# Reusing the first pair's stored weight operands in the second, and seven block products for the last down projection

## The chip, the cores and the metric

One core of one Trainium2 chip. The time is device microseconds of one execution of the whole program, from launch to the end. The four sequences of the problem are all computed on this core.

## The reference, cut to what matters

For each of 4 sequences x (512 rows by 512 features): attention with Wq, Wk, Wv, Wp gives `attn_out`; then a first two-layer block `cms = gelu(attn_out @ cW1 + cb1) @ cW2 + cb2 + onehot(code)`, a second one `modifier = gelu([attn_out, cms] @ mW1 + mb1) @ mW2 + mb2`, and `y0 = clip(x + cms + modifier, 0, 1)`. Both have 2048 hidden features; cW1 has 512 input rows, mW1 has 1024. After them come three small expert layers (512 to 256 to 512 with gelu, residual and layer norm), chosen for each sequence by an index. All is float32. The change touches the two blocks in the middle, called layer one (cW) and layer two (mW) here.

## The kernel before, in words

**Split arithmetic.** A float32 operand is held as a high part (a cast to the fast fp32r type, on ScalarE) and a low part (operand less high part, on VectorE), each of its own. Every product is three matmuls (`mm3`, L554 to L559): high times high, high times low, low times high. Data lie transposed, features on partitions.

**Pairs and chunks.** Sequences go in two pairs. For each pair the 2048 hidden features of a layer are done in four chunks, so a pair has eight chunks (`NCHUNK`): four of layer one, four of layer two; the two pairs have chunks 0 to 7 and 8 to 15 (`NCH` is 16). A chunk first does two quads of the up projection, then the down projection of what they gave (L702 to L705, with `up_quad` and `down_chunk`).

**Up projection by seven products.** A quad is a block matrix product of 2 by 2 blocks: two tiles of hidden features, two halves of the input features, two sequences. It is done with seven block products (P1 to P7, Strassen's way in Winograd's form) instead of eight; each is two steps of k, so 6 matmuls of 128 by 512. For this the weights are summed and split into seven operands of 128 partitions by 256 in high and low part (2 KB a partition). Layer two has twice the input features, so its quad has 14 operands. A chunk thus has 14 operand steps in layer one and 28 in layer two, 84 and 168 matmuls.

**How a weight operand is made.** SyncE loads a raw piece (`raw_piece`, L426, 512 KB), VectorE makes the sums (`weight_sums`, L1226), ScalarE the high part (`weight_hi`, L897), VectorE the low part (`weight_lo`, L1222), into a ring of six (`ring`, 192 KB to 204 KB of the partition). TensorE waits for `aop_lo` at each step and counts `aop_used` after it. The making runs five steps ahead (`AHEAD`). Both pairs use the same weights, and the whole of it is done again for the second pair.

**Down projection.** `down_chunk` (L690) takes eight steps d of 12 matmuls: four tiles of hidden features, two sequences, four output tiles, no sums, 96 matmuls in all. The weights of a tile are loaded raw (`down_weights`, L432, 256 KB), split by `down_weight_hi` and `down_weight_lo`; gelu's output is split by `g_hi` (L939) and `g_lo` (L1287) into three buffers. Down step d = 7 needs `g_lo(ci, 7)`, and ScalarE does `g_hi(ci, 7)` in its own d = 5, behind `weight_hi` of the next chunk's fifth operand in d = 4 (L1023 to L1031). Results are added into `res` by VectorE (`down_add`).

**SyncE's order.** All DMAs of the kernel are issued by SyncE, from one written-out order (L384 to L548): it waits for a semaphore, issues, and goes on to the next; what stands behind a wait waits too. At the change of pairs (chunk 7) it loads the second pair's seven row operands (`next_a_operand`, 1 MB each) and x of the first pair (`xs[0]`, 2 MB, L474). In chunk 9 it stores y0 of the first pair (2 MB, L477), and in chunk 11 that in split form (4 MB, L480). Near the end of chunk 15 it loads y0_split (2 x 2 MB), x of the second pair, y0 and the weights of the first expert units (L461 to L530), with twelve `unit_columns` of 5 KB each. At the start, behind the load of the expert indices, it begins a chain for the expert weights: load a piece (`prep`, L419), high part on ScalarE (`piece_hi`, L813), low part on GpSimd, store (L415); ScalarE does its parts between those of the attention (L847 to L851).

## Time and profile before

| | |
|---|---|
| median of 3 runs | 1193.47 us (1193.29 to 1194.72) |
| the profiled execution's own time | 1194.04 us |
| its span, first to last instruction | 1192.2 us |
| TensorE matmul busy | 1178.7 us, 99% |
| VectorE, ScalarE busy | 790.8 us (66%), 569.3 us (48%) |
| DMA, mean over the span | 122 GB/s, 145.82 MB |
| granted clock, mean | 0.999 of full |

The profiled execution's time is 0.57 us over the median; its span leaves 1.8 us of it outside the first and last instruction. Busy time of TensorE is modelled at its ends, so 99% says that it hardly ever stood idle.

### The profile page before, as it was taken

To read this page: it belongs to the slowest core of one execution; us is meant where nothing else is said; L and a number is where in the kernel's file an instruction comes from. 1 tells how busy PE (TensorE), PEld (TensorE's weight loads), DVE (VectorE), ACT (ScalarE), POOL (GpSimd) and SP (SyncE) were. 2 spreads that over 40 slices of the span, in tenths; PEclk is the share of its full clock that TensorE was granted. 3 is DMA by queue.
4 is the path that set the end of the run, shared out by engine and by line. 5 is a ranking of instruction groups with operands and counts; after the bars stand their busy time and mean duration, and the time that the engine had idled before them with its cause. 6 is when DMAs were issued, how large, how long until landed. Compare 5 with 4: busy or idle time off the path is not lost.

```text
span 1192.2 us, 15272 instructions
## 1 busy us (share of the span) xinstructions
PE 1178.7 (99%) x5328; PEld 973.9 (82%) x5328; DVE 790.8 (66%) x1460; ACT 569.3 (48%) x1068; POOL 162.5 (14%) x145
## 2 busy tenths in 40 slices
PE   9999999999999999999999999999999999999997
PEld 7888878888888788888888888878888888788886
DVE  6344486776678756565667686696656565877885
ACT  5434353563544534342435643554343434357886
POOL 1332230000000000000000000000000000349981
PEclk9999999999999999999999999999999999999999
DMA  6764452124320302020561321411111118746644
GB/s 226 273 216 161 164 175 94 54 60 153 124 96 28 107 13 95 10 98 8 194 258 53 124 62 45 178 53 53 54 53 54 54 36 326 223 142 224 218 167 169
DMA packets 50610, 145.82 MB, mean 122 GB/s; under 512 B 6356, under 2 KB 6356, under 8 KB 46310
## 3 DMA queue, kind: packets, MB, share of 16 engines
q1 hardware_dynamic: 50534, 144.84, 34.7%
q8 instruction: 43, 0.70, 0.2%
q14 instruction: 33, 0.27, 0.1%
HBM read 108.11 MB, written 36.71 MB: 121 GB/s over the span
## 4 chain that ended last, share of the span: by engine, by line
PE 92%; DVE 5%; issue 1%; DMA 1%; ACT 1%; POOL 0%; POOLq 0%; DVEq 0%; SPq 0%; ACTq 0%
PE psum L557 89%; PE psum L777 2%; DVE c_op L1334 1%; DVE res L1362 1%; DVE ring L1224 1%; DVE res L1307 1%; PE psum L608 0%; PE psum L591 0%; PE psum L721 0%; PE psum L604 0%; DMA wqk_raw<-wqk_dram 0%; DVE sm L1477 0%; DMA prep<-wdu_dram 0%; DVE z L1471 0%; DVE c_t L1319 0%
## 5 line engine op out<-in xcount | busy, mean ns | idle before, releaser
L557 PE MATMUL psum<-g_hl,w_hl 128*128 128x512 f32 x1536 | 351.3, 389 | 0.4 <-DVE w_hl L1285 0.4
L557 PEld LDWEIGHTS psum<-g_hl,w_hl 128*128 128x128 f32 x1536 | 288.1, 188 | 61.0 <-DVE w_hl L1285 0.8
L557 PE MATMUL psum<-a_op,ring 128*128 128x512 f32 x1344 | 316.7, 389 | 0.7 <-DVE w_t L1266 0.7
L557 PEld LDWEIGHTS psum<-a_op,ring 128*128 128x128 f32 x1344 | 252.1, 188 | 54.0 <-DVE w_t L1266 1.5
L906 ACT CAST ring<-asum 128x256 fp32r<-128x256 f32 x192 | 77.2, 404 | 210.5 <-PE psum L557 160.0
L557 PE MATMUL psum<-c_op,ring 128*128 128x512 f32 x672 | 163.9, 391 | 0.8 <-DVE c_op L1334 0.6
L557 PEld LDWEIGHTS psum<-c_op,ring 128*128 128x128 f32 x672 | 125.5, 188 | 29.4 <-DVE c_op L1334 3.6
L1292 DVE TENSOR_TENSOR g_hl<-g,g_hl 128x512 fp32r<-128x512 f32 x128 | 88.2, 689 | 67.9 <-ACT g_hl L946 66.5
L1553 POOL TENSOR_TENSOR yT<-res,yT 128x512 fp32r<-128x512 f32 x8 | 11.7, 1488 | 846.3 <-ACT yT L1044 846.3
L1224 DVE TENSOR_TENSOR ring<-asum,ring 128x256 fp32r<-128x256 f32 x192 | 80.5, 421 | 56.1 <-ACT ring L906 54.9
L946 ACT CAST g_hl<-g 128x512 fp32r<-128x512 f32 x128 | 78.3, 618 | 77.5 <-PE psum L557 77.5
L923 ACT ACTIVATE g<-g,sm 128x512 f32<-128x512 f32 x96 | 69.5, 724 | 78.8 <-DVE g L1272 31.5
L1224 DVE TENSOR_TENSOR ring<-rawp,ring 128x256 fp32r<-128x256 f32 x144 | 60.7, 423 | 62.8 <-ACT ring L906 61.6
L906 ACT CAST ring<-rawp 128x256 fp32r<-128x256 f32 x144 | 57.6, 404 | 55.3 <-PE psum L557 55.3
L1307 DVE TENSOR_TENSOR res<-psum,res 128x512 f32<-128x512 f32 x96 | 64.8, 691 | 20.2 <-PE psum L557 18.6
L557 PE MATMUL psum<-wu,h_hl 128*128 128x512 f32 x288 | 68.4, 393 | 0.0
L557 PE MATMUL psum<-yT,wd 128*128 128x512 f32 x288 | 67.8, 391 | 0.0
L1545 POOL TENSOR_TENSOR prep<-prep 128x512 f32<-128x512 f32 x36 | 50.2, 1401 | 126.4 <-ACT prep L817 126.4
L557 PEld LDWEIGHTS psum<-yT,wd 128*128 128x128 f32 x288 | 53.8, 188 | 11.1
L557 PEld LDWEIGHTS psum<-wu,h_hl 128*128 128x128 f32 x288 | 53.3, 188 | 10.7
L1285 DVE TENSOR_TENSOR w_hl<-wraw,w_hl 128x512 fp32r<-128x512 f32 x64 | 44.1, 689 | 20.3 <-ACT w_hl L937 19.3
L557 PE MATMUL psum<-vp_w,xT 128*128 128x512 f32 x192 | 45.3, 391 | 0.0
(128 smaller groups left out, 1352.7 us busy)
## 6 DMA issues: line engine op xcount, KB each, us to landing
rawp<-up_w_dram SPq DMA_DIRECT2D x48, 512.0 KB, 3.6
wdu_split<-prep SPq DMA_DIRECT2D x36, 512.0 KB, 2.9
wraw<-dn_w_dram SPq DMA_DIRECT2D x64, 256.0 KB, 3.3
wd<-wdu_split SPq DMA_DIRECT2D x12, 1024.0 KB, 9.1
wu<-wdu_split SPq DMA_DIRECT2D x12, 1024.0 KB, 5.4
prep<-wdu_dram SPq DMA_DIRECT2D x36, 256.0 KB, 3.3
second_pair_operands<-c_op SPq DMA_DIRECT2D x7, 1024.0 KB, 6.3
a_op<-second_pair_operands SPq DMA_DIRECT2D x7, 1024.0 KB, 11.7
```

What stands on the lines that cost most here:

```text
L557: ins = nc.tensor.matmul(ps, lw(el), rw(er), start=first and i == 0, stop=last and i == 2, skip_group_check=skip)
L777: ins = nc.tensor.transpose(tr_bank(u, d)[:, i * P:(i + 1) * P], z[u % 3][:, i, d * P:(d + 1) * P], ident[:, :])
L906: nc.scalar.copy(ring[n % RING][:, 0, :], aop_src(n)).then_inc(aop_hi, 1)
L923: nc.scalar.activation(dst, src, ACT.Gelu, bias=(cb1, mb1)[l][:, t:t + 1]).then_inc(gelu_done, 1)
L946: nc.scalar.copy(g_hl[t % GHL][:, 0, :], g[:, q, 2 * row + seq, :]).then_inc(g_hi_done, 1)
L1224: nc.vector.tensor_tensor(ring[n % RING][:, 1, :], aop_src(n), f(ring[n % RING][:, 0, :]), ALU.subtract).then_inc(aop_lo, 1)
L1285: nc.vector.tensor_tensor(w_hl[t % 2][:, 1, :], wraw[t % 2][:, :], f(w_hl[t % 2][:, 0, :]), ALU.subtract).then_inc(w_lo_done, 1)
L1292: nc.vector.tensor_tensor(g_hl[t % GHL][:, 1, :], g[:, q, 2 * row + seq, :], f(g_hl[t % GHL][:, 0, :]), ALU.subtract).then_inc(g_lo_done, 1)
L1307: nc.vector.tensor_tensor(dst, bank[4 * seq + m], dst, ALU.add).then_inc(d_evac, 1)
L1334: nc.vector.tensor_tensor(c_ops[i][:, 1, :, :], src, f(c_ops[i][:, 0, :, :]), ALU.subtract).then_inc(op_lo[2 + p], 1)
L1362: nc.vector.tensor_scalar(res[:, 2 + seq, m, :], res[:, 2 + seq, m, :], 0.0, 1.0, ALU.max, ALU.min).then_inc(y0_done, 1)
L1545: nc.gpsimd.tensor_tensor(prep[i][:, 1, :], prep[i][:, 1, :], prep[i][:, 0, :], ALU.subtract).then_inc(p_lo, 1)
```

## The change: what it does

1. In the first pair every weight operand of the up projection, once split, is also stored to DRAM (`store_operand`, 168 stores of 256 KB, 2 KB rows). Its slot in the ring may be filled again only when the store has landed.
2. In the second pair (chunks 8 to 15) these operands are not made again: `load_operands` brings two at a time into the ring (512 KB, 4 KB rows), when the two that were in their place have been used. TensorE waits for the landing.
3. In chunks 8 to 11 ScalarE and VectorE make instead the operands of mW2 for the block products of the down projection (56 of them) in four staging buffers, which are stored as well.
4. In chunks 12 to 15 the down projection is done by seven block products over 2 by 2 blocks: 14 steps of 6 matmuls (84) instead of 96; the row operands are sums of gelu's output (`g_sum`), split into eight buffers (`dg`); VectorE adds the products to `acc_u` and `res`. VectorE adds `acc_u` in at the end.
5. SyncE's order follows from this: stores in all chunks of the first pair and chunks 8 to 11, loads between them. x of the first pair is loaded in four parts in chunk 8 (steps k = 4 to 7), y0 stored in four in chunk 9 (k = 0 to 3), y0_split stored in eight of 512 KB in chunk 10 (k = 1 to 8); y0_split's second half comes after chunk 15's seventh down step. The twelve `unit_columns` are issued at the start, behind the expert indices. `x_add` and the clip of the second pair's y0 come after the first rows of y0.

The diff, cut to its core:

```diff
+CS = NCHUNK + NCHUNK // 2
+LOADED = AOP
+PREPARED = AOP + PROD * QL
+UP_OPS = QC * 2 * PROD
+DOWN_STEPS = (tuple((i, 0) for i in (P1, P6, P7, P5)) + tuple((i, 1) for i in (P1, P6, P7, P5))
+              + tuple((i, q) for i in (P2, P4, P3) for q in range(QC)))
+CSTEP = len(DOWN_STEPS)
+COPS = UP_OPS + CSTEP
+TOTAL = PREPARED + (NCH - CS) * COPS
+STG = 4
+DG = 8
+ADDS = (P1, P6, P7, P5, P2, P4, P3)
+ADD_BANK = (0, 2, 4, 6, 0, 4, 6)
...
+        ring_all = at("ring", 192, [P, RING, 2, 2 * P], F32R)
+        ring = [ring_all[:, i, :, :] for i in range(RING)]
+        stage = [at(f"stage{i}", 104 + 2 * i, [P, 2, 2 * P], F32R) for i in range(STG)]
+        t_x, t_y = (at(f"t_{n}", 120 + 4 * i, [P, QC, S]) for i, n in enumerate("xy"))
+        acc_u = at("acc_u", 172, [P, 2, S])
+        dg = [at(f"dg{i}", k, [P, 2, S], F32R) for i, k in enumerate((160, 164, 168, 144, 148, 152, 112, 116))]
+        xs = [at(f"xs{i}", k, [P, 2, DT, S]) for i, k in enumerate((56, 48))]
...
+        up_ops = nc.dram_tensor("up_operands", (AOP // 2, P, 2, 4 * P), F32).ap()
+        down_ops = nc.dram_tensor("down_operands", (PROD * QL // 2, P, 2, 4 * P), F32).ap()
...
+        G_SUM_UP = {2: ((0, 0),), 3: ((0, 1),), 4: ((0, 2),), 10: ((0, 3),)}
+        G_SUM_DOWN = {1: ((1, 0), (1, 1), (1, 2)), 5: ((1, 3),)}
+        G_OP_UP = {4: 0, 6: 1, 7: 2, 8: 3, 13: 4}
+        G_OP_DOWN = {1: (5,), 2: (6,), 3: (7,), 4: (8,), 5: (9,), 6: (10,), 7: (11,), 8: (12,), 9: (13,)}
+        ADD_AT = {5: 0, 6: 1, 7: 2, 8: 3, 10: 4, 12: 5}
...
+            for u in range(LAYERS * B):
+                unit_columns(u)
...
+            def store_operand(n):
+                sp.wait_ge(aop_lo, n + 1)
+                src = f(aop_dst(n)[:, :, :].rearrange("p e n -> p (e n)"))
+                if n < LOADED:
+                    sp.dma_start(up_ops[n // 2, :, n % 2, :], src).then_inc(s_wst[n % RING], 16)
+                else:
+                    i = down_place(n)
+                    sp.dma_start(down_ops[i // 2, :, i % 2, :], src).then_inc(s_dst[n % STG], 16)
+            def load_operands(r):
+                sp.wait_ge(aop_used, r - RING + 2)
+                down, i = loaded_from(r)
+                for k in range(2):
+                    if r < LOADED + RING:
+                        sp.wait_ge(s_wst[(r + k) % RING], 16 * (LOADED // RING))
+                    if down:
+                        n = made_as(i + k) - LOADED
+                        sp.wait_ge(s_dst[n % STG], 16 * (n // STG + 1))
+                    else:
+                        sp.wait_ge(s_wst[(i + k) % RING], 16 * ((i + k) // RING + 1))
+                sp.dma_start(f(ring_all[:, r % RING:r % RING + 2, :, :].rearrange("p a e n -> p a (e n)")), (up_ops, down_ops)[down][i // 2]).then_inc(s_ring[r % RING // 2], 16)
...
+                for n in range(first, first + ops):
+                    store_operand(n)
+                    pieces_after(n)
+                    if n == first + ops - 3:
+                        down_weights(4 * ci + 2)
...
+            for r in range(LOADED, LOADED + RING, 2):
+                load_operands(r)
+            for i in (P2, P4, P3):
+                next_a_operand(NCHUNK - 1, i)
+            def x_piece(k):
+                if k == 0:
+                    sp.wait_ge(aop_used, used_after(NCHUNK - 1, 1, P6))
+                sp.dma_start(xs[0][:, k // 2, k % 2 * 2:k % 2 * 2 + 2, :], xin[k // 2, :, k % 2 * 2:k % 2 * 2 + 2, :]).then_inc(s_xs[0], 16)
+            def y0_piece(k):
+                sp.wait_ge(y0_done, k + 1)
+                sp.dma_start(y0_dram[:, k // 2, k % 2 * 2:k % 2 * 2 + 2, :],
+                             xs[0][:, k // 2, k % 2 * 2:k % 2 * 2 + 2, :]).then_inc(s_spill, 16)
+            def y0_split_piece(k):
+                b, e, h = k // 4, k // 2 % 2, k % 2
+                sp.wait_ge(y0_lo_done, 2 * b + h + 1)
+                sp.dma_start(y0_split[b, :, e, 2 * h:2 * h + 2, :], f(y0_hl[:, b, e, 2 * h:2 * h + 2, :])).then_inc(s_y0split, 16)
+            for ci in range(NCHUNK, CS):
+                first, ops = aop_at(ci, 0), QC * PROD
+                down_weights(4 * ci)
+                down_weights(4 * ci + 1)
+                for k in range(-STG, ops):
+                    if k >= 0 and k % 2:
+                        load_operands(first + RING + k - 1)
+                    if k + STG < ops:
+                        store_operand(first + STG + k)
+                        pieces_after(first + STG + k)
+                    if ci == NCHUNK and 4 <= k < 8:
+                        x_piece(k - 4)
+                    if ci == NCHUNK + 1 and 0 <= k < 4:
+                        y0_piece(k)
+                    if ci == NCHUNK + 2 and 1 <= k < 9:
+                        y0_split_piece(k - 1)
+                    if k == ops - 3:
+                        down_weights(4 * ci + 2)
+                down_weights(4 * ci + 3)
+            def split_rows(b, e):
+                sp.wait_ge(aop_used, aop_at(NCH - 1, 1) + 2 + 2 * b)
+                sp.wait_ge(s_y0split, 16 * 8)
+                sp.dma_start(f(yT[b][:, e, :, :]), y0_split[b, :, e]).then_inc(s_yTin[b], 16)
...
+            last_up = aop_at(NCH - 1, 1)
+            for r in range(PREPARED + RING, TOTAL):
+                if r % 2 == 0:
+                    load_operands(r)
+                if r in (last_up + RING + 3, last_up + RING + 5):
+                    split_rows(0, (r - last_up - RING - 3) // 2)
+                if r == last_up + RING + 7:
+                    unit_down(0)
+                if r in (last_up + RING + 13, last_up + RING + 15):
+                    seq = (r - last_up - RING - 13) // 2
+                    sp.wait_ge(aop_used, last_up + LAYER_STEPS[1].index((P3, 0)) + 1)
+                    sp.dma_start(xs[1][:, seq, :, :], xin[2 + seq]).then_inc(s_xs[1], 16)
+                if r == last_up + RING + 16:
+                    for b in range(B):
+                        sp.dma_start(bup0[:, b, :], bup_all[bass.ds(ex[b], 1)].to_broadcast([P, V])).then_inc(t_bup0, 16)
+            sp.wait_ge(s_spill, 16 * 4)
+            sp.wait_ge(aop_used, dop_at(NCH - 1, 7) + 1)
             sp.dma_start(res[:, 0, :, :], y0_dram[:, 0]).then_inc(s_y0in[0], 16)
-            unit_down(0)
-            for b in range(B):
-                sp.dma_start(bup0[:, b, :], bup_all[bass.ds(ex[b], 1)].to_broadcast([P, V])).then_inc(t_bup0, 16)
-            sp.wait_ge(aop_used, PAIRS * AOP)
-            for u in range(LAYERS * B):
-                unit_columns(u)
             unit_up(0)
-            sp.wait_ge(w_lo_done, 4 * NCH)
+            unit_down(1)
+            for e in range(2):
+                split_rows(1, e)
+            sp.wait_ge(aop_used, dop_at(NCH - 1, 8) + 1)
+            sp.wait_ge(f_done, 3)
             sp.dma_start(res[:, 1, :, :], y0_dram[:, 1]).then_inc(s_y0in[1], 16)
-            unit_down(1)
             unit_up(1)
-            sp.wait_ge(d_used, 4 * DSTEP * NCH)
+            sp.wait_ge(aop_used, TOTAL)
...
+                    if n < LOADED:
+                        pe.wait_ge(aop_lo, n + 1)
+                    else:
+                        pe.wait_ge(s_ring[n % RING // 2], 16 * ((n - LOADED) // RING + 1))
...
+            def down_products(ci):
+                for step, (prod, q) in enumerate(DOWN_STEPS):
+                    r, t = dop_at(ci, step), CSTEP * (ci - CS) + step
+                    if q == 0:
+                        down_step_bank_free(ci, prod)
+                    pe.wait_ge(s_ring[r % RING // 2], 16 * ((r - LOADED) // RING + 1))
+                    pe.wait_ge(dg_lo, t + 1)
+                    for m in range(2):
+                        ins = mm3(bank[ADD_BANK[ADDS.index(prod)] + m], lambda e: ring[r % RING][:, e, m * P:(m + 1) * P],
+                                  lambda e: dg[t % DG][:, e, :], prod <= P5 and q == 0, q == QC - 1, skip=prod > P5)
+                    ins.then_inc(aop_used, 1)
...
+                if n < LOADED:
+                    if n >= RING:
+                        act.wait_ge(aop_used, n - RING + 1)
+                        act.wait_ge(s_wst[n % RING], 16 * (n // RING))
+                elif n < LOADED + STG:
+                    act.wait_ge(aop_used, LOADED)
+                else:
+                    act.wait_ge(s_dst[n % STG], 16 * ((n - LOADED) // STG))
+                nc.scalar.copy(aop_dst(n)[:, 0, :], aop_src(n)).then_inc(aop_hi, 1)
...
+            def g_op_hi(ci, step):
+                prod, q = DOWN_STEPS[step]
+                t, Q = CSTEP * (ci - CS) + step, QC * ci + q
+                if prod in (P1, P2, P3):
+                    act.wait_ge(gelu_done, 4 * Q + {P1: C11, P2: C21, P3: C22}[prod] + 1)
+                else:
+                    act.wait_ge(t_dsum, g_sum_count(ci, q, {P7: 0, P5: 1, P6: 2, P4: 3}[prod]))
+                if t == 0:
+                    act.wait_ge(aop_lo, PREPARED)
+                    act.wait_ge(d_used, 4 * DSTEP * CS)
+                if t >= DG:
+                    c, k = divmod(t - DG, CSTEP)
+                    act.wait_ge(aop_used, dop_at(CS + c, k) + 1)
+                nc.scalar.copy(dg[t % DG][:, 0, :], g_operand(q, prod)).then_inc(dg_hi, 1)
...
+            def down_product_add(ci, k):
+                dve.wait_ge(aop_used, step_done(ci, ADDS[k]))
+                if k >= 2 and ci == CS:
+                    dve.wait_ge(d_evac, 8 * CS)
+                if k == 0 and ci == CS:
+                    dve.wait_ge(s_accu, 1)
+                for m in range(2):
+                    last = {0: (ci - 1, 1), 1: (ci, 0), 2: (ci - 1, 3), 3: (ci, 2)}.get(k, (ci - 1, k))
+                    if last[0] >= CS:
+                        dve.wait_ge(e_done, e_count(*last, m))
+                    if ci == NCH - 1 and k in (5, 6):
+                        dve.wait_ge(f_done, {5: 2, 6: 3}[k])
+                    half = int(k in (2, 3, 5))
+                    dst = acc_u[:, m, :] if k < 2 else res[:, 3 if k in (2, 3, 6) else 2, 2 * half + m, :]
+                    if ci == CS and k in (2, 4, 5, 6):
+                        nc.vector.scalar_tensor_tensor(out=dst, in0=bank[ADD_BANK[k] + m], scalar=mb2[:, 2 * half + m:2 * half + m + 1],
+                                                       in1=dst, op0=ALU.add, op1=ALU.add).then_inc(e_done, 1)
+                    else:
+                        nc.vector.tensor_tensor(dst, bank[ADD_BANK[k] + m], dst, ALU.add).then_inc(e_done, 1)
...
+            def first_sum_add(i):
+                dve.wait_ge(e_done, e_count(NCH - 1, 3, 1))
+                seq, half = ((1, 1), (0, 1), (1, 0))[i]
+                dst = res[:, 2 + seq, 2 * half:2 * half + 2, :]
+                nc.vector.tensor_tensor(dst, acc_u[:, :, :], dst, ALU.add).then_inc(f_done, 1)
```

## Rows read from the trace of the kernel before

**Rows 1.** The page, part 1: busy time, share and instructions of each engine.

```profile
PE 1178.7 (99%) x5328; PEld 973.9 (82%) x5328; DVE 790.8 (66%) x1460; ACT 569.3 (48%) x1068; POOL 162.5 (14%) x145
```

**Rows 2.** The chain that ended last: start, length, what, count.

```profile
798.88 221.31 PE psum L557 x975
```

**Rows 3.** Busy time by stretch: stretch, its length, busy of each engine (instructions), clock, DMA share, GB/s.

```profile
776.00:799.00 23.00, 22.29 (x95) 17.02 (x94) 22.93 (x35) 11.92 (x22) 0.00 (x0) 1.00 0.20 68
799.00:1020.00 221.00, 221.00 (x975) 182.98 (x976) 136.00 (x267) 86.79 (x182) 0.00 (x0) 1.00 0.26 89
```

**Rows 4.** Timeline of TensorE, chunks 7 to 9: start, length, line, matmuls.

```profile
567.20 1.52 PE L557 MATMUL psum<-a_op,ring 128*128 128x512 f32 x6
568.56 1.52 PE L557 MATMUL psum<-c_op,ring 128*128 128x512 f32 x6
...
594.40 21.92 PE L557 MATMUL psum<-g_hl,w_hl 128*128 128x512 f32 x96
616.16 19.20 PE L557 MATMUL psum<-a_op,ring 128*128 128x512 f32 x84
635.20 21.92 PE L557 MATMUL psum<-g_hl,w_hl 128*128 128x512 f32 x96
```

**Rows 5.** DMA issues of the whole run: count, KB each, median us to landing.

```profile
rawp<-up_w_dram SPq DMA_DIRECT2D x48, 512.0 KB, 3.6
...
y_split<-y_hl SPq DMA_DIRECT2D x1, 4096.0 KB, 12.9
...
out_dram<-res SPq DMA_DIRECT2D x8, 256.0 KB, 2.2
```

**Rows 6.** As rows 3, a stretch in which the queue was never empty.

```profile
595.00:608.00 13.00, 13.00 (x60) 10.74 (x58) 7.46 (x16) 5.87 (x12) 0.00 (x0) 1.00 1.02 423
```

**Rows 7.** The wraw load issued between 591.4 and 592.0: time to landing.

```profile
wraw<-dn_w_dram SPq DMA_DIRECT2D x1, 256.0 KB, 9.7
```

**Rows 8.** The last a_op load, issued at 593.3 to 593.95: time to landing.

```profile
a_op<-second_pair_operands SPq DMA_DIRECT2D x1, 1024.0 KB, 15.0
```

**Rows 9.** Timeline of SyncE, chunks 7 and 8: start, length, line, DMAs.

```profile
602.07 5.77 SPq L435 DMA_DIRECT2D wraw<-dn_w_dram  x2
...
630.07 20.04 SPq L435 DMA_DIRECT2D wraw<-dn_w_dram  x4
```

**Rows 10.** Timelines of ScalarE and VectorE, end of chunk 8.

```profile
649.05 0.62 ACT L946 CAST g_hl<-g 128x512 fp32r<-128x512 f32 x1 [1.27 <-PE psum L557]
...
649.07 0.69 DVE L1285 TENSOR_TENSOR w_hl<-wraw,w_hl 128x512 fp32r<-128x512 f32 x1
...
650.61 0.69 DVE L1292 TENSOR_TENSOR g_hl<-g,g_hl 128x512 fp32r<-128x512 f32 x1
```

**Rows 11.** As rows 3, while bup (broadcast loads) filled the queue.

```profile
1011.00:1016.00 5.00, 5.00 (x24) 4.14 (x23) 3.56 (x4) 0.83 (x2) 0.00 (x0) 1.00 0.97 186
```

**Rows 12.** Timeline of TensorE behind chunk 15's end.

```profile
1020.70 1.91 PE L721 MATMUL psum<-ident,res 128*128 128x128 f32 x16
...
1022.36 5.73 PE L557 MATMUL psum<-yT,wd 128*128 128x512 f32 x24
...
1029.41 2.36 PE L721 MATMUL psum<-ident,res 128*128 128x128 f32 x16 [1.32 <-DVE res L1442]
```

**Rows 13.** Unit_columns' issues: ns minimum, median, maximum, first and last start.

```profile
L502 SPq DMA_DIRECT2D unit_columns<-pp_dram x12: 332/558/1986, 1004.7 to 1015.7; - x12
```

**Rows 14.** Timelines at the start: SyncE, ScalarE, TensorE.

```profile
18.70 0.83 SPq L419 DMA_DIRECT2D prep<-wdu_dram  x2
...
26.61 0.44 SPq L419 DMA_DIRECT2D prep<-wdu_dram  x1
...
30.21 0.62 ACT L817 CAST prep<-prep 128x512 fp32r<-128x512 f32 x1 [3.94 <-DMA prep<-wdu_dram]
...
47.60 0.68 ACT L822 ACTIVATE probs<-psum,sm 128x512 f32<-128x512 f32 x1
...
49.95 8.33 PE L557 MATMUL psum<-vp_w,xT 128*128 128x512 f32 x36
```

245 lines of the change are left out of this document (171 added, 74 removed).

## The prediction

> **What bounds the kernel now.** I read the page's busy times first [rows 1]: TensorE has matmuls in 99% of the span, VectorE is at 66%, ScalarE at 48%. The chain that ended last says the same of the stretch that the change rewrites: from 799 us it is one piece of 221 us of line 557's matmuls [rows 2]. The stretches agree: 799 to 1020 has no idle TensorE at all, and the switch of layers in the second pair (776 to 799) has 23.00 less 22.29 = 0.7 us [rows 3]. So work taken from VectorE and ScalarE gives nothing; matmuls taken away give their whole time, and each new wait of TensorE costs its whole time. The queue of SyncE's DMAs, a quarter busy there, is what the change loads, so that is where I look for waits.
>
> **Units.** A product of 6 matmuls starts 1.36 us after the one before (567.20, 568.56) [rows 4]; I call this a step. A matmul is 0.227 us, and chunk 7's 96 down matmuls take 616.16 - 594.40 = 21.76 us. An up projection of layer one takes 84 of them, 19.04 us. For the queue: in 595 to 608 it is never empty and moves 423 GB/s [rows 6], so 1 MB (1,048,576 bytes) takes 2.48 us. A lone load of 512 KB lands after 3.6 us, a store of 256 KB after 2.2, the 4 MB store after 12.9 [rows 5]; I take 2.3 us fixed and 2.48 for each MB (3.5 for 512 KB, 12.2 for 4 MB). The queue works in order: a wraw load of 256 KB, issued behind four a_op loads, took 9.7 us [rows 7].
>
> **Gained.** Chunks 12 to 15 do 84 down matmuls each instead of 96: 48 x 0.227 = 10.9 us. At the layer switch VectorE no longer makes ring operands between its row operands; the 0.7 us may go. Together 11.6. Down steps on VectorE (g_sum, g_op_lo, product adds, at 0.69 us for 512 columns [rows 10]) need up to 9 x 0.69 = 6.2 us before step 4 of the second quad and less than 1.36 a step later, so I cost them at nothing; without that cover they would cost what VectorE is late.
>
> **Loads in the steady state.** A pair of operands must land within four steps, 5.44 us, of the use of the old pair. It needs 3.6 alone, and 512 KB for each 2.72 us is 193 GB/s against 423. In chunks 12 to 14 the queue holds little else: nothing. In the first pair stores ask 193 GB/s, raw pieces some 55; a store has six steps (8.2 us) to land: nothing. Where more is queued, load n lands at (issue of the first of the run) + 2.3 + 2.48 x (MB queued up to it); the excess over its deadline is a stall.
>
> - **Chunk 8.** From load k = 1 (at 2.72 us of the chunk) to load k = 7, due at 12 steps = 16.3: four loads 2 MB, stores 1.5, a raw piece 0.5, three quarters of x 1.5; 5.5 MB land at 2.7 + 2.3 + 13.6 = 18.6. Stall 2.3.
> - **Chunk 9.** Up to load k = 5, due at 13.6: 1.5 + 1 + 0.5 + 1.5 (y0) = 4.5 MB, 16.2. Stall 2.6.
> - **Chunk 10.** The eight parts of y0_split, each step one, six of them (3 MB) ahead of load k = 7: 2 + 1.5 + 0.5 + 3 = 7 MB, 22.4 against 16.3. Stall 6.1.
> - **Chunk 11.** Loads and stores alone, 1 MB in 2.72 us: nothing.
>
> **Stores that ScalarE waits for.** The fifth staged operand (weight_hi in d = 4) waits for the store of the first, which SyncE issues behind two down_weights that wait for weights split in d = 2 and d = 4; behind it on ScalarE stands g_hi for d = 7. In chunk 7 the second wait ended at 607.8 [rows 9]. The a_op loads landed until 593.3 + 15.0 = 608.3 [rows 8]; three ring loads (1.5 MB), two wraw and the store (0.75 MB) come on top: 608.3 + 5.6 = 613.9, then two casts and a subtraction, 615.7. Down step 7 starts at 594.40 + 7 x 2.72 = 613.4. Stall 2.3. In chunks 8 and 9 that second down_weights came at 650.1 [rows 9] or so; store landed 653.0, g_lo 654.8 against 635.20 + 19.04 = 654.2, with VectorE busy before [rows 10]: 1 us each, 2 together.
>
> **Chunk 15.** Two halves of y0_split and a wd load (3 MB) between ring loads: the one due at 19.04 of the second quad lands at 5.44 + 2.3 + 12.4 = 20.1, stall 1.1. Later x (2 MB) and bup. Bup's broadcast rows moved 186 GB/s with the queue full [rows 11]: 5.6 us for its 1 MB. The load behind them, due at 32.6: 19.04 + 2.3 + 9.9 + 5.4 = 36.6, stall 4.0. Together 5.1.
>
> **Behind it.** y0, wu, wd, 2 MB of y0_split and y0's second part then follow: 1.3 + 6 x 2.48 = 16 us behind that load, 52.8. TensorE ends the chunk at 38.1 + 4.0, does 16 transposes and 24 matmuls and wants them at 49.2; stall 3.6, where before it was 1.3 [rows 12]. Cost 2.3.
>
> **Start.** Twelve unit_columns go ahead of the prep chain. Their issue took 332 to 1986 ns, median 558 [rows 13], there with a full queue; I take 0.5, 6 us. Prep 0 is issued at 24.7 instead of 18.7 [rows 14], prep 2 at 30.7 instead of 26.6 (that one had waited for something else). The exponentials stand behind piece 8 on ScalarE: 47.6 becomes 51.7, first one done 52.4, where TensorE takes that bank again at 49.95. Cost 2.5; from 0 to 7 with 0.33 or 0.94 us an issue.
>
> **Sum.** 2.5 + 2.3 + 2.3 + 2.6 + 6.1 + 2.0 + 5.1 + 2.3 = 25.2, less 11.6: +13.6. Against the profiled execution, 1194.04, this gives 1207.6; the median is 0.57 lower, so 1207. No term can be taken below nothing: a wait not there saves only the matmuls. The upper ends add 10.
>
> The Trainium skill (DMA: Bandwidth & Descriptors, Where 436 GB/s comes from) says that between HBM and SBUF a core is held to some 358 GB/s. The trace does not agree here (423). By the page chunk 10's 7 MB would take 20.5 us and its stall be 9, the sum some 10 us more.
>
> **Rivals.**
> *The queue keeps up* (faster). The loads' deadlines hold because landing is not bound to order or because stalls in a row share one backlog: then only the start and tail cost, some 0 to 4, and 1194 - 11.6 + 2 = 1184 comes out. For it: mean traffic in chunks 8 to 11 is under capacity, and the issues are spread in parts. Against: rows 7, and that bytes due in chunk 10 (7 MB in 13.6 us, 540 GB/s) exceed 423. It decides where stalls stay under 9.
> *Only the bytes count* (about even): chunk 10 at 6, chunks 8 and 9 and 15 at half, start and tail nothing: 6 + 2.5 + 2.5 + 2 - 11.6 = +1.4, 1195. Stalls move SyncE's later issues too, which thins the backlog.
> *The clock falls.* Stalls of 2 to 4 us each, close together in chunk 10, bring the granted clock to its lower level (1.2 GHz), where a matmul costs twice its 0.227: with 30 matmuls after each of four stalls, 27 us more, 1234. The trace has 1.00 everywhere around idle times up to 1.3 us; longer ones it does not show in the middle. The Trainium skill (TensorE: Matmul & The Clock Gate, Part 1) has the clock fall after idleness; no row here can show it.
>
> **Chances.** Forecast with its own range 1200 to 1214: 0.52. Queue keeps up: 0.22. Only the bytes count: 0.18 (a third of it faster, a third same, a third slower). Clock: 0.08. What a measurement can tell from no change is 0.2%, 2.4 us. Faster 0.22 + 0.06 = 0.28; same 0.06; slower 0.52 + 0.08 + 0.06 = 0.66. The range takes the three cases and leaves out the clock and the last of the gain: 1184 to 1215.
>
> **What would show it.** Right: TensorE idle 5 to 7 us in chunk 10's up projection, in three pieces, its releaser a DMA into the ring; 2 to 3 in chunks 8 and 9; about 4 before a late down step of chunk 15; DMA share 1.0 in these stretches; 5280 matmuls instead of 5328. Chunks 12 to 14 at (168 + 84) x 0.227 = 57.1 us each. Wrong, if chunk 10 is as long as chunk 11; if ring loads behind y0_split land in 4 us; if the first exponentials stay at 47.6.

## The result, and the profile after

The changed kernel takes 1238.21 us (median of 4 runs, 1237.65 to 1239.14) against 1194.10 (4 runs, 1193.29 to 1195.65) for the kernel before on the same chip: ratio 1.0369, interval 1.0351 to 1.0387. The side forecast was right, the size was not: 13 us slower were forecast, 44 came.

The page of the changed kernel, parts 1 and 6, to be held against [rows 1, 5]:

```profile
PE 1183.1 (96%) x5280; PEld 971.5 (79%) x5280; DVE 759.2 (61%) x1351; ACT 531.3 (43%) x964; POOL 160.5 (13%) x146
...
up_operands<-ring SPq DMA_DIRECT2D x168, 256.0 KB, 2.7
ring<-up_operands SPq DMA_DIRECT2D x84, 512.0 KB, 3.4
...
down_operands<-stage SPq DMA_DIRECT2D x56, 256.0 KB, 5.8
ring<-down_operands SPq DMA_DIRECT2D x28, 512.0 KB, 3.3
```

Read it with [rows 1] as a sum. The span went from 1192.2 to 1236.3, 44.1 more. Outside matmuls TensorE spends 1236.3 - 1183.1 = 53.2 us, before 13.5: 39.7 more. Its matmuls take 4.4 us more although 48 are gone, and these had cost 10.9: so the others take 15.3 us longer than they did before. 39.7 + 15.3 - 10.9 = 44.1.

Not all of the 15.3 us is clock. Take the busy time of each microsecond times what is missing of full clock there: that sums to 12.3 us in the changed kernel and to 1.5 in the one before, so the clock cost 10.8. The other 4.5 us are the ends of rows. Twelve matmuls between two waits count 2.97 to 3.2 us at full clock, in a stream 2.72, and some 18 waits cut rows in this way. So there are 40 us of waits, 4.5 of their edges and 11 of clock to be explained. The one odd row of part 6 is the stores of the staged down operands: 5.8 us to landing, where the same 256 KB from the ring takes 2.7.

What TensorE waited for, the view of waits (sum, times, longest):

```profile
PE psum L726 <- DMA ring<-up_operands: 14.3, 8, 3.5
PE psum L726 <- DVE g_hl L1537: 12.7, 3, 5.8
PE psum L726 <- DVE res L1645: 4.0, 2, 2.4
PE psum L930 <- DMA res<-y_spill: 3.7, 1, 3.7
PE psum L726 <- ACT probs L1031: 3.5, 1, 3.5
```

And where, the timeline of TensorE: down step 7 of chunks 7 and 8, the start of chunk 9, down step 7 of chunk 9, chunk 10's up projection, chunk 15 and behind it (compare [rows 4, 12]):

```profile
625.00 4.40 PE L726 MATMUL psum<-g_hl,w_hl 128*128 128x512 f32 x12 [5.85 <-DVE g_hl L1537]
...
674.08 3.02 PE L726 MATMUL psum<-g_hl,w_hl 128*128 128x512 f32 x12 [1.74 <-DVE g_hl L1537]
...
691.45 5.96 PE L726 MATMUL psum<-a_op,ring 128*128 128x512 f32 x18 [3.47 <-DMA ring<-up_operands]
...
727.90 5.49 PE L726 MATMUL psum<-g_hl,w_hl 128*128 128x512 f32 x12 [5.11 <-DVE g_hl L1537]
...
747.98 4.32 PE L726 MATMUL psum<-a_op,ring 128*128 128x512 f32 x12 [3.43 <-DMA ring<-up_operands]
753.33 3.20 PE L726 MATMUL psum<-a_op,ring 128*128 128x512 f32 x12 [1.03 <-DMA ring<-up_operands]
758.64 2.99 PE L726 MATMUL psum<-a_op,ring 128*128 128x512 f32 x12 [2.12 <-DMA ring<-up_operands]
...
1037.20 11.22 PE L726 MATMUL psum<-dg,ring 128*128 128x512 f32 x48 [1.17 <-DMA ring<-down_operands]
1050.78 4.58 PE L726 MATMUL psum<-dg,ring 128*128 128x512 f32 x12 [2.36 <-DVE res L1645]
1057.04 5.69 PE L726 MATMUL psum<-dg,ring 128*128 128x512 f32 x24 [1.68 <-DVE res L1645]
...
1073.65 1.97 PE L930 MATMUL psum<-ident,res 128*128 128x128 f32 x16 [3.71 <-DMA res<-y_spill]
```

Look at the lengths too, not only at the brackets: twelve matmuls take 2.97 us at full clock, and 4.40 and 5.49 behind the two longest waits. The stretches show the clock itself. The row of 1030 is the queue in chunk 15, and the last row is the clock behind the wait of 3.71 us:

```profile
622.00:625.00 3.00, 0.00 (x1) 0.00 (x1) 1.17 (x3) 1.63 (x4) 0.00 (x0) 0.50 0.45 171
625.00:628.00 3.00, 3.00 (x7) 2.42 (x8) 2.97 (x6) 0.00 (x0) 0.00 (x0) 0.51 0.25 90
640.00:655.00 15.00, 11.18 (x47) 8.18 (x46) 7.96 (x15) 9.03 (x17) 0.00 (x0) 1.00 1.03 416
...
728.00:735.00 7.00, 7.00 (x19) 5.58 (x20) 5.79 (x11) 0.00 (x0) 0.00 (x0) 0.59 0.00 0
...
1030.00:1066.00 36.00, 30.41 (x132) 23.96 (x131) 24.40 (x37) 8.35 (x14) 0.00 (x0) 0.95 1.01 359
...
1073.00:1079.00 6.00, 5.35 (x32) 4.75 (x33) 3.28 (x5) 0.76 (x2) 4.34 (x4) 1.00 1.02 255
```

The clock fell behind six waits, those of 3.46 us at 53.83, 5.85, 3.47, 5.11, 3.43 and 2.36 us, and cost 1.4 to 2.9 us behind each, 11.0 together. Behind the wait of 3.71 us it stayed full.

The wait before 625.00 names VectorE, but VectorE is only the last link. One engine back, the timeline of ScalarE:

```profile
623.29 0.41 ACT L1121 CAST stage<-rawp 128x256 fp32r<-128x256 f32 x1 [11.07 <-DMA down_operands<-stage]
623.61 0.61 ACT L1164 CAST g_hl<-g 128x512 fp32r<-128x512 f32 x1
```

ScalarE stood 11.07 us before the fifth staged operand, because its buffer was held by the first one's store; the g_hl that TensorE wanted stood behind it. And one further back, SyncE's timeline in chunk 7, where [rows 9] had the two wraw issues at 602.07:

```profile
591.58 2.61 SPq L536 DMA_DIRECT2D up_operands<-ring  x2
594.29 2.33 SPq L564 DMA_DIRECT2D a_op<-second_pair_operands  x4
...
597.58 2.88 SPq L553 DMA_DIRECT2D ring<-up_operands  x3
600.56 2.64 SPq L564 DMA_DIRECT2D a_op<-second_pair_operands  x3
607.62 5.77 SPq L558 DMA_DIRECT2D wraw<-dn_w_dram  x2
613.43 1.86 SPq L539 DMA_DIRECT2D down_operands<-stage  x4
```

The waits of 2.36 and 1.68 us in chunk 15 are put down to an addition on VectorE, yet end with landings: by the view of DMA issues the ring load of 1042.95 took 7.7 us to landing, until 1050.7, and the two behind the bias broadcasts 10.2 in the median, the first until 1057.0.

**A ledger by chunk** is what I used to compare kernels: the time at which a chunk's down projection starts in the trace (rows like 594.40 and 635.20 in [rows 4]), less that of the kernel before. It shows where time is lost and where it comes back. The last column is the end of the span, also less that of the kernel before.

```
start of the down projection of chunk     7     8     9    10    11    12    14    15   end
the changed kernel                      5.6  17.9  27.4  44.7  46.4  44.5  39.0  38.3  44.1
e1 fifth operand later                  5.0  13.6  20.2  31.2  32.8  30.9  25.4  24.9  33.5
e2 y0 transfers behind loads            6.7  18.2  25.9  33.3  39.6  37.6  32.2  31.3  37.9
e5 three moves                          0.3   6.5  12.5  17.2  19.1  17.1  11.7  12.6  19.3
e7 no stage stores                      4.7   6.6   9.2  13.8  13.8  11.9   6.4   5.9  11.5
e9 e5, residual late                    0.0   6.5  11.5  15.0  16.5  14.5   9.0   8.4  21.1
e11 y0 split in the tail                3.4   6.5  12.9  15.3  16.8  14.8   9.4   8.2  19.5
e12 that, no stage stores               2.3   2.3   3.6   3.6   3.6   1.7  -3.8  -5.0   6.6
e13 e11, eight buffers                  2.1   2.7   8.3   8.7   9.4   7.4   2.0   0.6  12.2
e14 e11, tail in order                  1.0   4.1   9.9  11.8  13.1  11.1   5.6   4.3  14.9
e15 eight buffers, tail in order        3.5   4.3   8.7   9.4   9.8   7.8   2.4   1.9  11.7
```

In the changed kernel 5.6 us go at the start, 12.4 between chunks 7 and 8, 9.5, 17.2 and 1.8 in the three chunks behind. Then 8 come back: 2.0 at the layer switch (chunk 12), 2.7 in each of the next two chunks, 12 matmuls each, and 0.8 in the one before chunk 15, whose waits take the rest. From there to the end 5.8 are lost again.

The ledger is that of one execution, and executions differ. Ten kernels with the same start, that of e3 below, come to chunk 7 between 0.0 and 3.5 us late. So where two kernels start apart by this much, that difference is not the edit's.

### The profile page after: what moved, and what is told of

Read it like the earlier page. It is cut to its first block, busy times and chain, and to the rows that moved or that the text cites. A ratio compares the mean times of both kernels' runs of the same rounds, so it can differ in the third digit from the quotient of the medians.

```text
span 1236.3 us, 15321 instructions
## 1 busy us (share of the span) xinstructions
PE 1183.1 (96%) x5280; PEld 971.5 (79%) x5280; DVE 759.2 (61%) x1351; ACT 531.3 (43%) x964; POOL 160.5 (13%) x146
## 4 chain that ended last, share of the span: by engine, by line
PE 78%; DMA 9%; DVE 7%; SPq 2%; issue 2%; ACT 2%; POOL 1%; POOLq 0%; DVEq 0%; ACTq 0%
PE psum L726 75%; DMA down_operands<-stage 3%; DMA ring<-up_operands 2%; DMA prep<-wdu_dram 2%; PE psum L986 2%; DVE g_hl L1537 1%; DMA res<-y_spill 1%; DMA experts<-experts_dram 1%; DVE c_op L1577 1%; PE psum L760 1%; DMA ring<-down_operands 1%; POOL prep L1867 1%; DVE a_op L1392 0%; SPq L493 0%; DVE sm L1796 0%
## 5 line engine op out<-in xcount | busy, mean ns | idle before, releaser
L726 PE MATMUL psum<-a_op,ring 128*128 128x512 f32 x1344 | 323.6, 393 | 17.0 <-DMA ring<-up_operands 14.3
L726 PE MATMUL psum<-g_hl,w_hl 128*128 128x512 f32 x1152 | 268.5, 394 | 13.1 <-DVE g_hl L1537 12.7
L726 PEld LDWEIGHTS psum<-g_hl,w_hl 128*128 128x128 f32 x1152 | 218.5, 190 | 60.9 <-DVE g_hl L1537 14.0
L1537 DVE TENSOR_TENSOR g_hl<-g,g_hl 128x512 fp32r<-128x512 f32 x96 | 66.1, 689 | 50.7 <-ACT g_hl L1164 49.5
L726 PE MATMUL psum<-dg,ring 128*128 128x512 f32 x336 | 79.1, 396 | 5.2 <-DVE res L1645 4.0
L1121 ACT CAST ring<-asum 128x256 fp32r<-128x256 f32 x96 | 38.5, 404 | 104.0 <-PE psum L726 76.0
L726 PEld LDWEIGHTS psum<-dg,ring 128*128 128x128 f32 x336 | 63.9, 191 | 19.9 <-DVE res L1645 4.8
L1164 ACT CAST g_hl<-g 128x512 fp32r<-128x512 f32 x96 | 58.5, 617 | 47.1 <-PE psum L726 47.1
L1148 ACT COPY u_t<-psum 128x512 f32<-128x512 f32 x32 | 18.7, 586 | 88.5 <-PE psum L726 88.4
L1469 DVE TENSOR_TENSOR ring<-asum,ring 128x256 fp32r<-128x256 f32 x96 | 40.1, 420 | 26.4 <-ACT ring L1121 25.8
L1550 DVE TENSOR_TENSOR res<-psum,res 128x512 f32<-128x512 f32 x72 | 47.4, 688 | 12.3 <-PE psum L726 12.2
```

What stands on the lines that cost most here:

```text
L726: ins = nc.tensor.matmul(ps, lw(el), rw(er), start=first and i == 0, stop=last and i == 2, skip_group_check=skip)
L1121: nc.scalar.copy(aop_dst(n)[:, 0, :], aop_src(n)).then_inc(aop_hi, 1)
L1148: nc.scalar.copy(u_t[:, :], bank[4 * q + BANK_OF[P1]]).then_inc(u_done, 1)
L1164: nc.scalar.copy(g_hl[t % GHL][:, 0, :], g[:, q, 2 * row + seq, :]).then_inc(g_hi_done, 1)
L1469: nc.vector.tensor_tensor(aop_dst(n)[:, 1, :], aop_src(n), f(aop_dst(n)[:, 0, :]), ALU.subtract).then_inc(aop_lo, 1)
L1537: nc.vector.tensor_tensor(g_hl[t % GHL][:, 1, :], g[:, q, 2 * row + seq, :], f(g_hl[t % GHL][:, 0, :]), ALU.subtract).then_inc(g_lo_done, 1)
```

## The experiments

Each ratio is against the kernel before, measured beside it, with its interval; gains are from medians of four to six executions and good to 2 to 4 us.

**e1: the next chunk's fifth operand two down steps later**, chunks 7 to 10, on ScalarE and VectorE.

```diff
-                    if d < AHEAD and ci + 1 < CS:
+                    if d < AHEAD - (ci >= NCHUNK - 1) and ci + 1 < CS:
                         weight_hi(aop_at(ci + 1, 0) + d)
+                    if d == AHEAD + 1 and NCHUNK - 1 <= ci < CS - 1:
+                        weight_hi(aop_at(ci + 1, 0) + AHEAD - 1)
...
```

> The changed kernel, but in chunks 7 to 10 the fifth staged weight operand of the next chunk is split in down step 6 on ScalarE and VectorE instead of in step 4, so that g_hi and g_lo of step 7 no longer stand behind its wait for a landed store. Theory A (that wait is what holds step 7): the three waits of 5.8, 1.7 and 5.1 us before the last 12 down matmuls of chunks 7, 8 and 9 go, and the lowered clock behind two of them with them, so 13 to 18 us less than the 1238.2 of the changed kernel. Theory B (the queue is the bound, and the wait only stands where it is seen): the late store holds the next quad instead, 0 to 6 us less.

1228.85 us, 1.0287 (1.0267 to 1.0307): 9.4 less, between the two theories. All three waits before down step 7 are gone; by chunk 15 the ledger is 13.4 lower, and 2.8 of these are given back from there on (the wait for the last ring loads is 4.12 instead of 1.68). So the held buffer does reach TensorE by this way, for about the sum of those waits; it is not the larger part.

**e2: x, y0 and the parts of y0_split behind the ring loads of their chunks** (from k = 8 on).

```diff
-                    if ci == NCHUNK and 4 <= k < 8:
-                        x_piece(k - 4)
-                    if ci == NCHUNK + 1 and 0 <= k < 4:
-                        y0_piece(k)
-                    if ci == NCHUNK + 2 and 1 <= k < 9:
-                        y0_split_piece(k - 1)
+                    if ci == NCHUNK and 8 <= k < 12:
+                        x_piece(k - 8)
+                    if ci == NCHUNK + 1 and 8 <= k < 12:
+                        y0_piece(k - 8)
+                    if ci == NCHUNK + 2 and k >= 8:
+                        y0_split_piece(k - 8)
...
```

> The changed kernel, but the four parts of x in chunk 8, the four of y0 in chunk 9 and the eight of y0_split in chunk 10 are issued from k = 8 on, behind the last ring load that the same chunk's up projection needs. Theory A (megabytes ahead of a ring load, in order, set its landing): no TensorE wait for a ring load of over 1 us in chunks 8 to 10; there are 15 us of them and some 6 us of lowered clock, so 14 to 21 us less than 1238.2. Theory B (the queue is over its capacity for the chunk as a whole): the backlog goes into the down projection, the staged stores land later, step 7 waits longer than 5 us, and 0 to 8 us are won.

1231.21 us, 1.0291 (1.0259 to 1.0323): 7.0 less, theory B. The view of waits says where the gain stayed:

```profile
PE psum L729 <- DVE g_hl L1540: 17.4, 5, 6.6
...
PE psum L729 <- DMA ring<-up_operands: 1.0, 3, 0.4
```

The ring loads' waits fell from 14.3 us to 1.0, those for g_hl rose from 12.7 to 17.4. Of these, the waits before down step 7 are 6.61, 2.74, 3.83 and 2.40, so 15.6: the bytes that no longer stand ahead of loads stand ahead of the staged stores. The fifth, 1.84 us in chunk 8, has another cause, which the edit made. x now lands late, VectorE stands 2.73 us before its first addition of the residual, and g_lo stands behind that. So this edit frees the loads and holds the g_hl. Of e1 the same can't be said: its waits for ring loads fell too, from 14.3 to 11.4 us, and new ones came, 3.8 for additions on VectorE and 1.8 for g.

**e3: the twelve column loads behind the last store of expert pieces** (issued at 182 us) instead of ahead of the prep chain.

> The changed kernel, but the twelve unit_columns are issued behind the last wdu_split store, where SyncE waits anyway. Theory A (they delay the chain of expert pieces, and ScalarE's exponentials behind it): the first down projection starts at 229.7 us as in the kernel before, not at 235.3, and the whole is 5.6 us less, 1232.6. Theory B (the start is held by something else, as the longer first load of the indices): within 1.5 us of 1238.2.

1233.43 us, 1.0316 (1.0298 to 1.0334): 4.8 less, nearer to theory A. TensorE's wait for the exponentials (3.46 us at 53.83) is gone. But the profiled execution is the slowest of the four (1237.60), and of the start's 5.6 us in the ledger 3.0 still stand in it; some 2 of them come in the first 11 us, where eight of its first matmuls took 3.16 us instead of 2.02. Over all kernels: five without this edit come to chunk 7 between 4.7 and 6.7 us late, 5.7 in the mean, and ten with it 0.0 to 3.5, 2.1 in the mean. So the columns cost some 3.6 us, and 2 have another cause, which no run isolates.

**e4: stalls put into the kernel before**, to price the clock alone. Memsets on GpSimd hold one ring operand back; nothing else changes.

```diff
+            for n, count in STALLS:
+                pool.wait_ge(aop_used, n)
+                for _ in range(count):
+                    nc.gpsimd.memset(sm[:, 196:224], 0.0).then_inc(s_gate, 1)
...
+                    if n in GATES:
+                        pe.wait_ge(s_gate, GATES[n])
```

> The kernel before, with TensorE made to wait for a chain of small GpSimd memsets at six places of the second pair: one of 10 memsets in chunk 9, one of 20 in chunk 10, one of 40 in chunk 11, and three of 10 with two operand steps between in chunk 13. 
1223.40 us, one run. TensorE's timeline of this kernel, a stall in chunks 9, 10 and 11 and three in chunk 13:

```profile
664.11 13.87 PE L560 MATMUL psum<-a_op,ring 128*128 128x512 f32 x60 [1.93 <-POOL sm L1562]
708.90 16.45 PE L560 MATMUL psum<-a_op,ring 128*128 128x512 f32 x60 [3.72 <-POOL sm L1562]
759.83 16.55 PE L560 MATMUL psum<-a_op,ring 128*128 128x512 f32 x60 [7.28 <-POOL sm L1562]
...
932.60 2.69 PE L560 MATMUL psum<-a_op,ring 128*128 128x512 f32 x6 [1.93 <-DVE ring L1229]
...
939.11 2.42 PE L560 MATMUL psum<-a_op,ring 128*128 128x512 f32 x6 [1.93 <-POOL sm L1562]
```

and three of its stretches, behind the 1.93 in chunk 9, the 3.72, and the first 1.93 in chunk 13:

```profile
664.00:668.00 4.00, 3.89 (x17) 3.27 (x18) 1.29 (x3) 2.04 (x5) 0.00 (x0) 1.00 0.01 2
...
709.00:713.00 4.00, 4.00 (x10) 3.13 (x11) 0.43 (x1) 1.12 (x3) 0.00 (x0) 0.50 0.00 0
...
933.00:936.00 3.00, 3.00 (x9) 2.33 (x8) 1.00 (x3) 0.40 (x1) 0.00 (x0) 0.50 0.04 18
```

It takes 29.2 us more than the kernel before, in the range expected. Sixty matmuls need 13.9 us behind the stall in chunk 9 and 16.5 behind one of 3.72 or 7.28: 2.6 us more, the same for both. Behind the long ones the granted clock is 0.50, which is 1.2 instead of 2.4 GHz. In chunk 13 the clock fell behind all three stalls of 1.93 us, and already behind the first, which was as lone as that of chunk 9. With 5.8 us of idling the three add 11.4 us to this kernel's ledger (18.6 at chunk 13, 30.0 at chunk 14). Of the 5.6 beyond the idling, 0.3 for each go without any clock (chunk 9's stall adds 2.2 us in all), so 4.8 are the clock's. So the length of a stall alone does not say whether the clock falls: 1.93 us left it full once and brought it down once here, and 3.71 us left it full at the changed kernel's 1073.65. Where it fell, the cost was of the same size, 1.4 to 2.9 us.

**e5: the three moves together**, the edits of e1, e2 and e3 in one kernel.

> The three moves of the earlier experiments in one kernel: the next chunk's fifth operand two down steps later, the first pair's residual and y0 transfers behind the ring loads of their chunks, and the twelve column loads behind the first piece stores. Theory A, the three waits are separate: the gains add, 9.4 + 7.0 + 4.8 = 21.2 us less than the changed kernel, 1217 us. Theory B, the first two relieve the same backlog on the one queue, so that part of each gain is the other's: 12 to 16 us less, 1222 to 1226. Theory C, each relieves what held the other back (the loads of chunks 8 to 10 and the steps that wait for staged operands): more than 24 less, under 1214.

1212.38 us, 1.0150 (1.0129 to 1.0171): 25.8 less than the changed kernel, where the single gains add to 21.2. By its number this is theory C, but three medians add up to an error as large as the difference, and the ledger speaks for theory A: from chunk 7 to chunk 11 e1 saves 13.1 us, e2 8.0 and this kernel 22.1. Only theory B is out. The waits for ring loads fall to 3.1 us and those for g_hl to 1.5, and in their place TensorE waits 4.1 us for additions on VectorE.

**e6: the bias broadcasts behind the last two ring loads.**

```diff
-                if r == last_up + RING + 16:
-                    for b in range(B):
-                        sp.dma_start(bup0[:, b, :], ...)
+            for b in range(B):
+                sp.dma_start(bup0[:, b, :], ...)
             sp.wait_ge(s_spill, 16 * 4)
```

> The four broadcast loads of the tail's bias stand behind the last two ring loads instead of ahead of them; nothing else moves. In the changed kernel these loads landed at 1056.95 and 1058.24, and TensorE's steps of chunk 15 stood 2.36 and 1.68 us. Theory A, the broadcasts are what made the last ring loads late: those two waits shrink to under 1 us together, and the time falls by 2 to 5 us. Theory B, the queue is behind by then whatever its order and the tail needs the bias as urgently (VectorE adds it at 1064.59): the wait only moves behind the down projection and the time stays within 1.5 us.

1241.30 us, 1.0387 (1.0369 to 1.0404): 3 more, outside both theories, and nearer to B. The waits of chunk 15 did shrink (2.36 and 1.68 became 0.77 and 0.78), but TensorE now waits for both residuals behind it:

```profile
PE psum L929 <- DMA res<-y_spill: 7.7, 2, 3.9
```

where the changed kernel waits once, 3.7 us, and full clock was lost behind both (2.38 and 3.68 us for the 16 transposes, instead of 1.91 and 1.97).

**e7: no stores of the staged down operands.** The ring loads that fetched them bring stored up operands of the same size, so the kernel leaves out part of the work and the second pair's values are others.

```diff
-                    sp.dma_start(down_ops[i // 2, :, i % 2, :], src).then_inc(s_dst[n % STG], 16)
...
-                    act.wait_ge(s_dst[n % STG], 16 * ((n - LOADED) // STG))
+                    act.wait_ge(aop_lo, n - STG + 1)
```

> Leaves out the 112 stores of layer two's prepared down operands (their ring loads fetch stored up operands in their place, same sizes), so the values of the second pair's layer two are others; SyncE still waits for each operand as before, and ScalarE waits for VectorE's pass over a staging buffer instead of for its store. Theory A, the stores' places in the one queue, and the buffers held until they land, are the cost: the waits in chunks 7 to 10 before step 7 vanish and the ring loads land in time, 25 to 35 us less than the changed kernel, 1203 to 1213. Theory B, what holds the queue is SyncE's waiting for operands in order and the residual and y0 transfers: 0 to 10 less, over 1228.

(There are 56 such stores, not the 112 of the expectation.) 1208.91 us, 1.0129 (1.0112 to 1.0145): 29.3 less, theory A. All waits for g_hl are gone. So 56 stores of 256 KB, 14 MB in a queue that is not full on average, are worth two thirds of the loss, with the buffers that they hold; e13 tells the two apart. The rest is in the ledger: 4.7 at the start, 9.1 in chunks 7 to 10, and 5.6 from chunk 15's down projection on.

**e8: e5 with the bias behind the last ring loads.**

> The three moves and the bias behind the last ring loads, together. Theory A, the bias's gain is separate from the others: 2 to 5 us below the kernel with the three moves. Theory B, in the tail the queue is behind whatever its order: within 1.5 us of it. No theory expects it under the 1194 us of the kernel before: even 26 us less is 1212.

1213.89 us, 1.0159 (1.0142 to 1.0176): 1.5 more than e5, theory B.

**e9: e5 with the second pair's residual late**, its two loads behind the first spilled residual.

> The kernel with the three moves, and in it the last chunk's two 1 MB loads of the second pair's residual behind the first spilled residual, where they are wanted; they stood between the last seven ring loads. In the kernel with the three moves TensorE stands 1.02, 0.33 and 4.21 us in chunk 15's down projection. Theory A, the bytes ahead of the last ring loads are what stalls it: these 5.6 us of waits fall under 2, the tail gives back at most one, and the time is 2.5 to 5 us below that kernel. Theory B, as the bias's move showed, the queue has more to bring from chunk 15 on than it can by the time it is wanted, and the wait only moves to the rows behind: within 1.5 us of it.

1215.83 us, 1.0190 (1.0171 to 1.0210): 3.4 more than e5, nearer to theory B, but slower than it had. Chunk 15's waits fell from 5.6 us to 4.8 and this one grew, from 2.81:

```profile
1047.52 3.67 PE L931 MATMUL psum<-ident,res 128*128 128x128 f32 x16 [8.21 <-DMA res<-y_spill]
```

That row starts at 1047.36 in e5 and at 1047.52 here, though e9's chunk 15 began 4.2 us earlier. The landing that it waits for comes when the queue has moved what stands ahead of it, in whatever order. From chunk 15's down projection to the end this kernel loses 12.7 us and e5 6.7. All kernels from here on keep this move; none was measured without it.

**e10: as e9, the fifth operand at the next chunk's first step** in chunks 8 to 11 (`weight_hi(n + AHEAD - 1)` at position 0 instead of in down step 6).

> As the kernel before it in this call, but the next chunk's fifth operand is split at the chunk's first step and not in down step 6, in chunks 8 to 11. With it in step 6 TensorE stood 2.73 us at the start of chunk 8 and 1.34 in chunk 10, both put down to VectorE's additions of the down projection, which stand behind that split. Theory A, the split still waits for a store there and holds the additions: both waits go, 3 to 6 us less than the kernel with the residual late. Theory B, the fifth operand comes too late for the chunk's fifth step or its ring loads: within 1.5 us of it, or slower.

1212.01 us, 1.0147 (1.0116 to 1.0177): 3.8 less than e9, theory A. The wait of 2.55 us at chunk 8's start for VectorE's additions is gone.

**e11: e10 with y0 split in the tail.** Chunk 9's split, chunk 10's eight stores and the tail's four loads of y0_split fall away; ScalarE and GpSimd split the reloaded residual.

```diff
-                    if ci == NCHUNK + 2 and k >= 8:
-                        y0_split_piece(k - 8)
-            for e in range(2):
-                split_rows(1, e)
...
+            y0_hi(0)
...
+                    y0_hi(1)
                     y0_hi(2)
-            for b in range(2, B):
+            for b in range(B):
                 for d in range(DT):
```

> On the kernel with the fifth operand split in its chunk: the first pair's y0 is no longer split in chunk 9, stored in chunk 10 (eight stores, 4 MB) and loaded in the tail (four loads, 4 MB); ScalarE and GpSimd split both rows from the reloaded residual in the tail, as they do for the second pair. In that kernel TensorE waits 7.09 us for the second residual, 1.34 and 4.43 us in chunk 15's down projection, and the queue lands one thing behind the other from chunk 15's middle on. Theory A, in the tail it is the bytes on the one queue that set the time: 4 MB at about 0.42 MB per us are 9 to 10 us that the queue gets back, and 7 to 11 us come off, 1201 to 1205. Theory B, the waits are those of the order, and the new splits on the way to the first rows cost what is won: within 2 us of it.

1212.34 us, 1.0140 (1.0123 to 1.0156): level with e10, theory B's number. The second residual's wait fell from 7.09 to 2.84 us; then the rows waited for GpSimd, in the timeline of GpSimd

```profile
1042.34 12.06 POOL L1870 TENSOR_TENSOR yT<-res,yT 128x512 fp32r<-128x512 f32 x8 [7.38 <-ACT yT L1282]
```

1.5 us a tile, and VectorE stood 5.04 us behind it. Chunks 8 to 11 did not gain (the ledger of e10 is 2.1, then 14.4; of e11 3.4, then 16.8): behind the ring loads, y0_split had cost them nothing any more.

**e12: e11 without the staged stores.**

> The kernel before it in this call without the stores of the prepared down operands (stored up operands are loaded in their place, so the values of layer two of the second pair are others). What is left of the change is then the stored operands' loads, the seven products and the extra sums. Theory A, these stores' landing is still what chunks 7 to 10 lose (12 us by the ledger of the kernel with the fifth operand in its chunk, of which the one with no stores kept 9): 3 to 8 us less than the kernel before it, 1194 to 1201, so that even without them the change wins nothing on the 1194 us of before. Theory B, without y0's traffic the stores are covered: within 1.5 us of it. Theory C, without both the 8 us of matmuls come through: under 1190.

1200.09 us, 1.0044 (1.0030 to 1.0057): 12.3 less than e11, more than theory A's 8. Chunks 8 to 11 now lose 1.4 us together, and by chunk 15 the kernel is 5.0 ahead of the one before. It ends 6.6 behind in the profiled execution, 5.4 by the medians: 11.6 us go in chunk 15's down projection and the rows after it. Like e7, this kernel leaves out the stores and computes other values.

**e13: e11 with eight staging buffers**, in the memory that the split y0 had held. Order and bytes of the queue are the same.

```diff
-STG = 4
+STG = 8
+ORDER = 4
...
-                for k in range(-STG, ops):
+                for k in range(-ORDER, ops):
```

> On the kernel that splits y0 in the tail: eight staging buffers for the down operands instead of four (the memory that the split y0 held), with the order of every queue unchanged, so the same 112 stores stand at the same places. There ScalarE stands up to 3.54 us before a staging buffer until its store of four operands before has landed, and TensorE loses 6 to 7 us in chunk 8's and 9's ledgers, 13 us by chunk 11; without the stores all but 1.4 of it is gone. Theory A, it is the buffer held until the landing, 4 to 8 us behind the issue, that hands the queue's lateness to ScalarE and back to SyncE: with eight buffers the ledger of chunks 8 to 11 falls under 5 us and the time by 7 to 11, 1201 to 1205. Theory B, the stores' bytes ahead of the ring loads in the queue are the cost, however many buffers: within 2 us.

1206.13 us, 1.0094 (1.0075 to 1.0112): 6.2 less than e11, a little under theory A's 7 to 11. ScalarE's waits, first e11:

```profile
ACT stage L1111 <- DMA down_operands<-stage: 42.2, 24, 8.3
```

In e13 there is no such row, only the one for the sums, which was there before (e11: 16.0):

```profile
ACT stage L1112 <- DVE asum L1480: 18.0, 8, 7.0
```

Chunks 8 to 11 cost 7.2 us in the ledger instead of 13.4, and without any stores 1.4. So of what the stores cost in this setting, 12.0, half is the held buffer (theory A's mechanism), and half remains with the bytes and places in the queue.

Most of that other half lies in chunk 8, 5.5 us in the ledger, and the timelines of VectorE and TensorE show where:

```profile
646.94 1.23 DVE L1578 TENSOR_TENSOR xs<-res,xs 128x1024 f32<-128x1024 f32 x1 [4.87 <-DMA xs<-x_dram]
...
648.82 3.06 PE L719 MATMUL psum<-g_hl,w_hl 128*128 128x512 f32 x12 [2.58 <-DVE g_hl L1533]
```

VectorE stands before its first addition of the residual until x has landed, and the g_lo that TensorE wants stands behind that addition. TensorE waits 2.58 us for it, 0.52 for w_hl and 1.25 for two ring loads of chunk 9. In the changed kernel VectorE has no such wait: it came with e2's move of x behind the ring loads. Without the staged stores (e12) it is 2.5 us instead of 4.9, and TensorE waits 0.23.

**e14: e11 with the tail in order**: bias behind the last two ring loads, the first pair's low halves on VectorE.

> On the kernel that splits y0 in the tail: the bias broadcasts behind the last two ring loads, and the low halves of the first pair's two rows made by VectorE (0.6 us a tile) instead of GpSimd (1.3 us a tile). There TensorE waits 3.48 us for the last ring loads and 2.84 for the second residual, and rows wait for GpSimd's passes afterwards (2.91 and 0.60). Theory A, with 4 MB less in the queue its order counts again, and the GpSimd passes were what gave the gain back: 4 to 8 us less, 1204 to 1208. Theory B, as when the bias was moved alone, the wait goes to the rows: within 2 us.

1208.58 us, 1.0110 (1.0091 to 1.0129): 3.8 less than e11, a little under theory A's range, but the ledger doesn't bear theory A out. Of the 4.6 us between the two profiled executions 2.4 stand at chunk 7 already and 1.4 come in chunks 7 to 10, all ahead of anything that was moved; from chunk 15's down projection to the end it loses 10.6 us and e11 11.3. So the tail gained some 0.7 us, theory B, and GpSimd's passes were not what kept e11's gain back. The down projection of chunk 15 now runs without a break (84 matmuls in 19.29 us), but the rows wait 5.74 and 3.68 us for the two residuals.

**e15: both.**

> Both of the other two in one kernel; its output is the whole reference. If theory A holds for both, the gains add, 11 to 19 us less than the kernel that splits y0 in the tail: 1193 to 1201, so level with the kernel before at best and not clearly under its 1194. If only one holds, 1201 to 1208; if neither, 1212.

1203.04 us, 1.0067 (1.0051 to 1.0083): 9.3 less than e11, where the two alone make 6.2 and 3.8; the time is in the range given for one theory alone. It is the best that computes the whole reference, 35 us below the changed kernel, and still 7.5 above the one before. The profiled execution's span is 11.7 longer: 3.5 at the start, 6.3 in chunks 7 to 10, minus 7.9 from the layer switch and the seven products, and 9.8 in chunk 15's down projection and the rows.

## Why the prediction was right in its side and wrong in its size

**The gain** came as worked out. From chunk 12 on the ledger falls by 2.72 us a chunk, 12 x 0.227; 5280 matmuls; the layer switch gave 1.97 instead of 0.7. VectorE's extra down steps cost nothing before chunk 15.

**Ring loads in chunks 8 to 10**, forecast 2.3 + 2.6 + 6.1 = 11.0: measured 1.16 + 0.84 + 1.82 = 3.8, then 3.5, then 3.43 + 1.03 + 2.12 = 6.6, together 13.9. The rule behind it held: landings follow the order of issue, at some 416 GB/s while the queue is full.

**Chunk 15**, forecast 5.1: 0.39 + 1.17 + 2.36 + 1.68 = 5.6, the bias broadcasts at the place and near the price given (the sum takes 5.4 us for them where its own price is 5.6). **The tail**, forecast at 3.6 us of waiting: 3.71.

**The start**, forecast 2.5: 5.6. Twelve issues took 7.2 us, not 6, TensorE waited 3.46 us, and the clock behind that wait was down (0.88 in 48 to 62), which I had not priced. By e3 some 3.6 of the 5.6 are the columns'.

**The stores that ScalarE waits for** are the first step that failed. Forecast 2.3 + 1 + 1 = 4.3, measured 5.85 + 1.74 + 5.11 = 12.7. In chunk 7 I let the a_op loads go out when they did before. They stand behind the stores of the last operands, which wait for VectorE; the first went out at 594.29, 8.7 us later than the 585.61 before, of which only 5.6 are the kernel's own lateness; the last, behind ring loads by then, landed after 19.8 us instead of 15.0 [rows 8]. The store of the first staged operand, at 613.43 behind them, took 9.8 us. In chunk 9 I took a lone store. It was the first of four issued 0.5 us apart, at 719.76 right behind a wraw load, and took 5.4 us; the view of DMA issues there:

```profile
down_operands<-stage SPq DMA_DIRECT2D x4, 256.0 KB, 5.6
```

The deeper fault: I priced each wait by itself against a queue that keeps its issue times. But a late landing holds a buffer, which holds ScalarE, then VectorE, then SyncE, which waits for that operand ahead of its next loads. The rows of chunk 7 show the first links of this loop, e2 that relieving one side loads the other, e7 that 29 us hang on the stores, and e13 that with more buffers, at the same order and bytes, half of what is left of that goes. That the links also multiply each other isn't shown: e5's parts add up, by the ledger, to what it gained.

**The clock** is the second and, by a little, the larger: forecast at nothing, with its own rival at 8 in 100 and 27 us. Measured 10.8 us. It is neither the rival (the mean granted clock is still 0.987) nor nothing. The prediction said that no row of the kernel before could show the fall. Its trace has one, behind waits of 2.36 and 0.67 us at the very end:

```profile
1186.00:1188.00 2.00, 2.00 (x11) 2.00 (x11) 0.81 (x1) 0.83 (x2) 0.00 (x0) 0.50 0.06 22
```

The Trainium skill (TensorE: Matmul & The Clock Gate, Part 1) has the clock fall after idleness; here the trace agrees, with 0.51 behind the wait of 5.85 us and 0.59 behind that of 5.11, though it stayed at 1.00 behind that of 3.71. What the forecast lacked was a price for one stall's clock: 1.4 to 2.9 us in the changed kernel, 2.6 in e4.

So of the 30.5 us missed, 10.8 are the clock, 4.5 the edges of the waits, 8.4 the staged stores, 2.9 the ring loads, 1.0 the waiting at the start (3.5 less 2.5), and 1.5 are 0.68 and 0.80 us in chunk 9 behind ScalarE and VectorE, for which the forecast had no term. The other terms were each off by 1.3 us or less, and some 2 us I did not place.

The rivals: *the queue keeps up* and *only the bytes count* fell, since the waits came where bytes were due. The HBM limit of the Trainium skill (DMA: Bandwidth & Descriptors, Where 436 GB/s comes from) did not show: 416 GB/s in 640 to 655, against its 358. Only in chunk 15, with broadcasts in it, did the full queue fall to that size (359), and [rows 11] show that these rows are slow by themselves.

What stays open: 2 us of the start, why 4 MB less in the tail gained so little (e11, e14), what e10 to e15 would take with e5's place for the second pair's residual and an earlier x, and whether any order of the tail's loads comes to the time before. No order tried did.

## What to carry to other kernels

Where one in-order queue carries stores whose buffers another engine waits for, don't price each wait alone: follow the loop landing, buffer, engine, issue, and give the buffers the depth of the queue's worst landing time, not of a lone store's. Add a price for the clock behind each stall of TensorE, here 1.4 to 2.9 us on top of its length wherever the clock fell, and don't count on a short stall to be free of it. When the last stage has more bytes to bring than time, moving one transfer mostly chose who waits here (e6, e8, e9, e14); whether bringing bytes earlier helps was not tried. And when kernels are built on each other, take back a move that measured slower before the next is added: e9's stayed in all that followed.

## What the runs showed that I had not expected

A stall of 7.28 us cost no more clock than one of 3.72 (16.55 and 16.45 us for 60 matmuls), and two lone stalls of the same 1.93 us in one execution differ: behind one the granted clock stayed at 1.00, behind the other it fell to 0.50. Four stores of 256 KB issued 0.5 us apart behind a single wraw load landed after 5.6 us each in the median, against 2.2 for a lone one [rows 5]. And GpSimd took 1.5 us for a tile that VectorE subtracts in 0.69 [rows 10], yet giving two of the rows back to VectorE (e14) hardly shortened the tail.
